# A graph-network kernel on one core: TensorE signals four times a group of edges, not seven, in the second loop over dst-ordered edges

## What is computed

```python
h = relu(layernorm(x))                       # layer 0: attention
hw = (h @ W.T).reshape(N, 4, 32)
att = leaky_relu(sum(hw[src] * a_src, -1) + sum(hw[dst] * a_dst, -1))
x = x + segment_sum(att[..., None] * hw[src], dst)
h = relu(layernorm(x))                       # layer 1: gated messages
row, col = src, dst
edge_input = concat([h[row], h[col], edge_attr])          # 384 wide
m = relu(edge_input @ W_weight + b_weight)
m = m * sigmoid(edge_input @ W_gate + b_gate)
out = x + segment_sum(m, row)
```

## Time and profile before

| | us |
|---|---|
| median of three runs | 6881.06 |
| lowest, highest | 6870.08, 6926.85 |
| the profiled execution, its own time | 6804.04 |
| its span on the core | 6802.3 |
| second loop in dst order, first to last scatter of L602 | 3301.0 to 5885.8 |
| mean granted TensorE clock, share of full speed | 0.806 |

### The profile page before, as it was taken

One profiled execution on the slowest core, in us unless ns is written; L12 is line 12 of the kernel. 1 busy time (PEld: TensorE's weight loads), 2 busy tenths in 40 slices (PEclk: granted clock), 3 DMA queues, 4 the chain that ended last, 5 costly groups with the idle time before them and its releaser, 6 DMA issues.

```text
span 6802.3 us, 115484 instructions
## 1 busy us (share of the span) xinstructions
PE 4586.3 (67%) x31443; PEld 3571.3 (53%) x31443; DVE 3200.8 (47%) x6951; ACT 1977.2 (29%) x4132; POOL 3646.0 (54%) x3908
## 2 busy tenths in 40 slices
PE   4455555555555555556878888787888788788884
PEld 3244444444444444444566666666666666566663
DVE  5555555555555555557411111111111111399996
ACT  3011111111111111113422222222222222478873
POOL 5255555555555555551466666666666666544442
PEclk7667766777776767768988888888888888899997
DMA  5122222222222222223544444444444444699998
GB/s 158 25 54 55 57 54 54 55 59 56 54 56 54 55 53 57 56 53 113 193 138 136 137 138 135 138 137 136 140 135 138 138 139 134 202 319 322 326 318 316
DMA packets 457999, 866.29 MB, mean 127 GB/s; under 512 B 122767, under 2 KB 276057, under 8 KB 457701
## 3 DMA queue, kind: packets, MB, share of 16 engines
q1 hardware_dynamic: 215031, 439.00, 21.1%
q0 software_dynamic: 177312, 379.95, 20.0%
q10 hardware_dynamic: 65620, 46.95, 2.1%
HBM read 558.92 MB, written 313.00 MB: 128 GB/s over the span
## 4 chain that ended last, share of the span: by engine, by line
PE 40%; issue 19%; DVE 17%; another core or an unknown queue 15%; DMA 6%; ACT 1%; DVEq 1%; SPq 1%; ACTq 0%; POOL 0%; POOLq 0%
PE ps L843 12%; PE ps L841 12%; DMA rows<-parts 5%; PE ps L828 3%; PE ps L764 3%; DVE msg L1444 3%; DVE to_node L1318 2%; PE ps L707 2%; DVE hot L1334 2%; DVE gat L1551 2%; PE ps L675 1%; DVE picked L1414 1%; PE ps L720 1%; DVE run_parts L1426 1%
## 5 line engine op out<-in xcount | busy, mean ns | idle before, releaser
L602 POOL DMA_INDIRECT parts<-rows,sidx x1664 | 1636.4, 983 | 960.8 <-issue 509.5
L1314 DVE TENSOR_SCALAR to_edge<-ps,iota_p 128x1024 bf16<-128x1024 f32 (+1 forms) x417 | 535.3, 1284 | 2079.6 <-remote 1832.2
L843 PE MATMUL ps<-nodes_w,to_edge 128*128 128x256 f32 x3328 | 1123.1, 412 | 225.4 <-issue 220.1
L764 PE MATMUL ps<-msg,to_node 128*128 128x128 f32 x3328 | 721.8, 395 | 803.4 <-DVE msg L1444 481.9
L841 PE MATMUL ps<-w_edge,gat 128*128 128x256 f32 x3328 | 1115.8, 411 | 210.0 <-issue 205.6
L584 POOL DMA_INDIRECT gat<-table,sidx x832 | 789.8, 949 | 798.3 <-DVE sidx L1326 428.4
L764 PEld LDWEIGHTS ps<-msg,to_node 128*128 128x128 f32 x3328 | 658.5, 298 | 852.1 <-issue 851.5
L584 POOL DMA_INDIRECT rows<-table,sidx x832 | 788.7, 948 | 587.4 <-DVE sidx L1326 298.3
L841 PEld LDWEIGHTS ps<-w_edge,gat 128*128 128x128 f32 x3328 | 682.0, 206 | 422.0 <-issue 313.6
L843 PEld LDWEIGHTS ps<-nodes_w,to_edge 128*128 128x128 f32 x3328 | 685.5, 207 | 401.5 <-issue 308.4
L1045 ACT ACTIVATE rows<-ps 128x512 f32<-128x512 f32 x832 | 467.5, 604 | 1385.4 <-remote 690.9
(11 more groups left out here) (231 smaller groups left out, 6503.3 us busy)
## 6 DMA issues: line engine op xcount, KB each, us to landing
rows<-parts SPq DMA_DIRECT2D x208, 1028.0 KB, 7.6
ea<-in_edge_attr SPq DMA_DIRECT2D x422, 256.0 KB
nodes_w<-table_b SPq DMA_DIRECT2D x208, 128.0 KB
parts<-rows,sidx POOLq DMA_INDIRECT x1664
nodes_w<-table_a SPq DMA_DIRECT2D x416, 64.0 KB, 5.2
gat<-table,sidx POOLq DMA_INDIRECT x832
rows<-table,sidx POOLq DMA_INDIRECT x832
x1w<-x ACTq DMA_DIRECT2D x208, 64.0 KB
```

The costliest lines, as they stand in the source:

```text
L602: nc.gpsimd.indirect_dma_start(out=parts, out_offset=bass.IndirectOffsetOnAxis(ap=sidx[:, s, j:j + 1], axis=0), in_=rows[:, s, j, :], in_o ...
L764: mmi = pe.matmul(out_ps, to_node[:, s % 2, j * P:(j + 1) * P], msg[:, s % 2, j * F:(j + 1) * F], start=(j == 0), stop=(j == J - 1))
L843: mmi = pe.matmul(z, to_edge[:, s % 2, j * P:(j + 1) * P], nodes_w[:, s, :], start=False, stop=True)
L1314: return nc.vector.tensor_scalar(to, spread.rearrange("p b n -> p (b n)"), iota_p[:], None, ALU.is_equal)
```

## The change

`turn_edges` signals `ea_tp` once, after all eight transposes, and both evictions of the turned attributes wait for that signal. `edge_products` signals `z1_up` after every second bank, so that the evictions of banks 0 and 1 wait for the first of two signals and those of banks 2 and 3 for the second. The counts that SP, VectorE and ScalarE wait for are halved to match. TensorE's waits for `part_up` and `ea_t`, ScalarE's signals, GpSimd's waits, and the number and order of all matmuls, copies and DMAs stay as they are.

```diff
@@ SP, load_window; and the same at the end of a pass
-                sp.wait_ge(z1_up, 4 * (U * turn + s + 1))
+                sp.wait_ge(z1_up, 2 * (U * turn + s + 1))
@@ TensorE, turn_edges
                     for j in range(4 * h, 4 * h + 4):
                         mmi = pe.transpose(ps[:, 2 + h, (j % 4) * P:(j % 4 + 1) * P],
                                            ea[:, s, j * F:(j + 1) * F], ident[:])
-                    mmi.then_inc(ea_tp, 1)
+                mmi.then_inc(ea_tp, 1)
@@ TensorE, edge_products
                         mmi = pe.matmul(z, to_edge[:, s % 2, j * P:(j + 1) * P], nodes_w[:, s, :],
                                         start=False, stop=True)
-                    mmi.then_inc(z1_up, 1)
+                    if k % 2 == 1:
+                        mmi.then_inc(z1_up, 1)
@@ ScalarE, evict_turned and evict_rows
-                    act.wait_ge(ea_tp, 2 * q + h + 1)
+                    act.wait_ge(ea_tp, q + 1)
-                    act.wait_ge(z1_up, 4 * U + 4 * q + k + 1)
+                    act.wait_ge(z1_up, 2 * U + 2 * q + k // 2 + 1)
@@ VectorE, at the start, and before by_node
-            dve.sem_inc(z1_up, 4 * U)
+            dve.sem_inc(z1_up, 2 * U)
-                        dve.wait_ge(z1_up, 4 * U + 4 * q)
+                        dve.wait_ge(z1_up, 2 * U + 2 * q)
```

More of the change, by code:

```diff
@@ L426, in _ @@
                 for s in range(U):
-                    sp.wait_ge(z1_up, 4 * (U * (w * GU + GU) + s + 1))
+                    sp.wait_ge(z1_up, 2 * (U * (w * GU + GU) + s + 1))
                     sp.sem_inc(past_waits, 1)
```

## The result

| | before | after |
|---|---|---|
| median of 12 runs, us | 6874.69 | 6898.85 |
| lowest, highest, us | 6816.85, 6926.85 | 6869.02, 6963.28 |
| ratio to before, 95% interval | | 1.006 (1.0035 to 1.0085) |
| span of the profiled execution | 6802.3 | 6878.8 |
| second loop, first scatter's start to last one's end | 2585.8 | 2610.5 |

The change gained nothing. The medians differ by 24 us, 0.35%, and the ratio is 0.6% on the slower side. A second comparison of the same two kernels gave 1.0019 (0.9992 to 1.0046). About 1% is what a comparison of this kernel with itself can't tell from nothing, so a small loss is likely but not shown. The forecast was 6731 us, 150 less than before.

What follows compares the result with a forecast made beforehand. The prediction took GpSimd's scatter, waiting about 440 us for late TensorE signals, to bound the second loop. Waits falling to 291 us save 150, other edits cost 0: 6881 - 150 = 6731 us, range 6580 to 6890.

Steps and rivals of the forecast that it cites:

- What bounds the loop: Second loop: GpSimd's DMAs set a floor of 10.3 us a group; late TensorE signals add 2.1 of waits, about 440 us.
- Cost of the edits on TensorE, ScalarE, VectorE and SP: Second loop: fewer signals free 0 us in TensorE's stream; later evictions of turned and product banks are covered, cost 0.
- The 16 us: TensorE in the second loop: the skill's 26.3 ns an increment, three fewer in each of 208 groups, estimated 16 us saved.
- What GpSimd gets from a batch: GpSimd's scatter: five signals still pass, carrying more banks; batches grow from 16 to 20 DMAs, 83 waits, 150 us less.
- A: Second loop: the number of signals doesn't matter, GpSimd's activity alone holds them back; gain 0, 6881 us; chance 0.22.
- B: GpSimd's scatter: pairing makes it stop after every group, 728 us of waits, 288 more, 7169 us; chance 0.13.
- C: Second loop: signals keep up with the DMAs, 440 us less, 6441 us; chance 0.10 together with a halfway case.
- Evictions in twos: ScalarE's product evictions L1045 would come in twos if the forecast was right.
- Waits down to 80 to 105: GpSimd's scatter L602: waits for L1045 would fall from 153 to some 80 to 105, at 3.5 to 4 us each.
- Products at 1.4 us rare: TensorE in the second loop: slowed products, one in 1.4 us, would become rare.
- The clock up: TensorE's granted clock in slices 20 to 35 would rise.
- Stretches of 20 DMAs: GpSimd's scatter: stretches of 20 DMAs without a wait would appear.

## Why the prediction was wrong

**What bounds the loop: the pattern right, the cause not.** GpSimd's pace of 1.29 us a DMA, TensorE's 8.2 us a group, and signals that arrive late while GpSimd scatters and together when it stops: the runs without the scatter gave 8.19 us a group with prompt signals, and those in the 5446 session gave 10.3. But the prediction took the other 2.1 us a group for waits for signals, and 10.3 for a floor that signals can bring the loop to. With four increments between the DMAs the banks were ready 38 us ahead and the loop took 12.43 us a group all the same. By this reading the 440 us weren't for TensorE's signals to give back.

**Cost of the edits on TensorE, ScalarE, VectorE and SP: right** as far as seen. The first turned bank's delay and SP's and VectorE's waits left no trace. TensorE's product records stand 0.216 us apart at full pace with seven signals a group and with nineteen, so three fewer bring its stream nothing: on that point the row's reading (0 us) holds. The 16 us by the Trainium skill's "TensorE: Matmul & The Clock Gate", section "The cost: per-tile semaphore tail", aren't seen; at its 26.3 ns the twelve more would make an estimated 66 us, and the loop's lengths are 2585.2 and 2585.8. It isn't a test of the 26.3 ns, since TensorE isn't what bounds the loop (8.2 us of work in 12.4).

**What GpSimd gets from a batch: the step that failed.** It had two assumptions, and each was wrong. First, "Suppose that as many signals get through a batch as before". Signals aren't what gets through. The share of them was 43, 40 and 39% with 7, 4 and 19 a group (28% with 3, by the whole group); four signals of one bank became two of two. The prediction itself named this as what would make its main term wrong, and took the number "as fixed from one batch", in which the rate of signals and the rate of banks can't be told apart. Second, a wait was priced at 3.5 us however long the batch before it. The rows already spoke against it: the earlier trace rows has a wait of 4.50 after sixteen DMAs, one of 3.29 after twelve. Had I sorted the waits by the DMAs ahead of them, I would have found 2.50 us after ten, 2.98 after twelve, 3.38 after fourteen and 4.41 after sixteen, about a quarter of a us for each. (Short stretches fit less well: the waits after the 43 of up to eight DMAs are of 1.9 to 3.3 us, by length.) Then no lengthening of the batches could have been expected to gain much. The run without L843 did lengthen them to sixteen and gained 0.06 us a group. The batch of sixteen wasn't the usual one either: 21 of the 162 waits come after sixteen DMAs, and the mean stretch is 10.2. By the sum's own batches the kernel before would have had 104 waits, not 153.

**The rivals.** A, that the number doesn't matter, came true, but not for its reason: it said the flush alone decides; really the sum of the waits follows the number of DMAs. I gave it 0.22. B described what one signal a group does, a stop after each group, with a price far too high, since it too used a fixed wait: with `z1_up` once a group the stretches are of 8.4 DMAs, and the waits, less the usual 0.30 each, sum to 521 us, not 728. C was wrong: signals never kept up. If the 0.6% is real, it may be what the pairing costs in small, since mean waits are 3.57 us against 3.03 and the loop is 0.1 us a group longer; no run shows that as the reason.

**The forecast's signs in the profile.** Evictions in twos: yes. Waits down to 80 to 105: no, 148. Products at 1.4 us rare: no, 242 steps of 1.2 to 1.7 us against 340 before. The clock up: no, 0.864 over the loop in both. Stretches of 20 DMAs: none; the longest are 16.

## What to carry to other kernels

When an engine waits often, sort its waits by what went before each of them, ahead of multiplying a count by a mean. If the wait grows with the stretch before it, the stretch is running up a debt, and fewer, longer stretches save nothing. What a wait ends with needn't be what it costs: a run in which the awaited thing is ready long before tells whether the time was its to give back. And when several things cross a boundary together (signals, banks, instructions), one stretch can't say which of them is rationed; a run with more of one of them and nothing else changed can.

## What the runs showed of the hardware

- While GpSimd issues indirect DMAs one after another, 27% of the product banks' signals are raised within 0.8 us of their matmul; with SP's plain DMAs of the same bytes in their place all are, whether GpSimd makes fills or does nothing.
- It isn't TensorE's signals alone: of GpSimd's own semaphore increments between such DMAs (17 ns as a rule) 595 of 6653 took over 200 ns.
- A debt of about 0.26 us an indirect DMA, made up in waits, over nine kernels, whether GpSimd waits for a bank or, with banks ready 38 us ahead, on its own instructions. With 0.9 us or more between the DMAs no wait was left, and 95 to 99% of signals were prompt.
- All of it belongs to a condition of the machine that comes and goes: on the same chip the kernel before took 5446 us in one session and 6978 in another. In the first, three kernels that differ from it on TensorE alone ran the loop at GpSimd's 1.29 us a DMA with no wait at all. What the condition is, and how small a gap would be enough under it, stays open.
